# A three-layer transformer kernel on one core: zero fills, first weights and rows on other queues, and odd heads copied by ScalarE

## The reference

```python
# layer 0: focused attention, then a gated mixture of 8 experts, top 2, capacity 560
slot = jnp.where(kept, experts * C + pos, E * C)
buf = jnp.zeros((E * C + 1, D), x.dtype).at[slot].set(xf[tokens])
gu = jnp.einsum('ecd,efd->ecf', xb, w12)
h = jax.nn.silu(g) * u
yb = jnp.einsum('ecf,edf->ecd', h, w3)
...
# layer 2: attention with 16 heads of 64, then 8 experts, top 2, no capacity
y = jax.nn.gelu(flat @ w1[e].T + b1[e], approximate=False)
out = out + y * cw[:, None]
...
return _layernorm(out, ln_w, ln_b)
...
# layer 3: attention with 16 heads of 16 (the narrow one)
scores = jnp.where(mask[:, None, :, :] == 0, jnp.float32(-1000000000.0), scores)
attn = jax.nn.softmax(scores, axis=-1)
```

## Time and profile before

| | us |
|---|---|
| median of 3 runs | 2884.37 (2881.86 to 2885.04) |
| the profiled execution | 2856.36, span 2854.6 |
| PE busy | 2507.7 (88%) |
| DVE busy | 1375.6 (48%) |
| ACT busy | 1158.1 (41%) |
| POOL busy | 801.9 (28%) |

### The profile page before, as it was taken

The page is one execution under the profiler, slowest core; times in us unless marked ns, Lnnn a source line. Parts: engine busy times, 40 slices in busy tenths (PEclk is TensorE's granted clock), DMA queues, the critical chain, the costliest instruction groups (busy, mean ns, idle before and its releaser), DMA issues. The chain is left out here.

```text
span 2854.6 us, 46446 instructions
## 1 busy us (share of the span) xinstructions
PE 2507.7 (88%) x15874; PEld 1765.5 (62%) x15874; DVE 1375.6 (48%) x4867; ACT 1158.1 (41%) x2651; POOL 801.9 (28%) x867
## 2 busy tenths in 40 slices
PE   5999786999986897979999999979899878889776
PEld 4766445888863454647765656556799746656544
DVE  6998511222215654546653333435011078887665
ACT  4556231111107992224444343423333346566331
POOL 3444140000005220017764444514000132222242
PEclk8999897999998998989999999989999969999898
DMA  4232365222105210044210000033888610000000
GB/s 139 76 114 99 122 185 167 90 90 91 53 17 151 69 56 1 1 114 142 109 55 12 7 12 6 1 132 111 298 326 327 241 33 18 18 15 9 1 7 20
DMA packets 71602, 252.17 MB, mean 88 GB/s; under 512 B 16299, under 2 KB 31944, under 8 KB 54912
## 3 DMA queue, kind: packets, MB, share of 16 engines
q1 hardware_dynamic: 61656, 225.71, 23.0%
q0 software_dynamic: 9744, 23.87, 2.8%
HBM read 197.44 MB, written 52.10 MB: 87 GB/s over the span
## 5 line engine op out<-in xcount | busy, mean ns | idle before, releaser
L2889 PE MATMUL L_ffne_up<-L_ffne_xT,L_ffne_wu 128*128 128x128 f32 (+1 forms) x2144 | 390.5, 337 | 7.0 <-DMA L_ffne_wu<-in_L_ffn_up 6.8
L2889 PEld LDWEIGHTS L_ffne_up<-L_ffne_xT,L_ffne_wu 128*128 128x128 f32 x2144 | 328.3, 193 | 54.3 <-DMA L_ffne_wu<-in_L_ffn_up 7.6
L1141 POOL TENSOR_SCALAR L_xattn_p<-L_xattn_p,L_xattn_rec 112x375 f32<-112x375 f32 x256 | 311.8, 1225 | 0.0
L1529 PEld LDWEIGHTS L_xattn_pt<-ident,L_xattn_p 112*125 112x125 f32 x1536 | 202.5, 194 | 164.2 <-issue 78.9
L1529 PE MATMUL L_xattn_pt<-ident,L_xattn_p 112*125 112x112 f32 x1536 | 254.0, 295 | 39.9 <-DVE L_xattn_pt L1378 36.2
L2874 PE MATMUL L_ffne_dn<-L_ffne_wd,L_ffne_hT 128*112 128x256 f32 (+1 forms) x1200 | 266.3, 379 | 1.5 <-issue 1.5
L1361 DVE TENSOR_REDUCE L_xattn_least<-L_xattn_s 112x1 f32<-112x375 f32 x256 | 128.3, 543 | 284.7 <-PE L_xattn_s L1517 284.5
L1378 DVE COPY L_xattn_pt<-L_xattn_pt 125x336 f32<-125x336 f32 x448 | 210.3, 498 | 68.9 <-PE L_xattn_pt L1529 65.7
L2874 PEld LDWEIGHTS L_ffne_dn<-L_ffne_wd,L_ffne_hT 128*112 128x112 f32 (+1 forms) x1200 | 216.8, 183 | 39.7 <-issue 2.1
L2777 POOL DMA_DIRECT2D L_ffn_ybuf<-L_ffne_y x75 | 40.1, 535 | 673.1 <-DVE L_ffne_y L2827 412.2
L1249 ACT ACTIVATE L_xattn_p<-L_xattn_s,L_xattn_least 112x375 f32<-112x375 f32 x256 | 145.1, 570 | 186.2 <-DVE L_xattn_least L1361 186.1
(11 more groups left out here) (364 smaller groups left out, 4509.0 us busy)
## 6 DMA issues: line engine op xcount, KB each, us to landing
L_ffne_wd<-in_L_ffn_down SPq DMA_DIRECT2D x43, 1024.0 KB, 4.8
L_ffne_wu<-in_L_ffn_up SPq DMA_DIRECT2D x35, 1024.0 KB, 5.3
L_ffne_wu<-in_L_ffn_up SPq DMA_DIRECT2D x8, 2048.0 KB, 7.5
L_xattn_kd<-L_xattnkvks SPq DMA_DIRECT2D x8, 1500.0 KB, 7.1
L_xattn_vd<-L_xattnkvvs SPq DMA_DIRECT2D x24, 500.0 KB
L_xattn_kt<-L_xattn_kd SPq DMA_DIRECT2D x8, 1500.0 KB, 6.8
L_xattn_v<-L_xattn_vd SPq DMA_DIRECT2D x8, 1500.0 KB
L_ffn_xbuf<-L_ffnr_zeros SPq DMA_DIRECT2D x8, 1120.0 KB, 13.1
```

The costliest lines, as they stand in the source:

```text
L1141: p = pool.tensor_scalar(at_p(b, head), at_p(b, head), rec[:, h, head:head + 1], None, ALU.mult)
L1529: m = pe.transpose(pt_ps[head % 2][0:KP, 0, kt * S:(kt + 1) * S], at_p(b, head)[:, kt * KP:(kt + 1) * KP], ident[0:S, 0:S])
L2889: m = pe.matmul(up_ps[s % RING][k][:, 0, 0:RH], wu[:, h, c, k * FF + f * 128:k * FF + (f + 1) * 128], xT[:, h, c, q * RH:(q + 1) * RH], st ...
```

## The change

Six things change. (a) The zero fills are issued by ACT, from a 320-column zero tile that lives through the whole program: those of layer 0 in the focused attention at batches 5, 7, 9 and 11, those of layer 2 in the wide attention at batches 8 to 11. xbuf is set up for the whole program, and POOL waits for the fills as before. (b) In routing of layer 0 SP issues wu and wd of expert 0 in the place where the fills stood, into buffers that are held from the program's start. (c) SLOTS is 2. (d) Rows of blocks 0 and 1 of both expert stages are issued by ACT at the stage's start. (e) In the narrow attention ACT copies all odd heads, so each PSUM bank has one engine that empties it. (f) At its start ACT loads the root's table beforehand, on a tiny input, and the bias is added behind the first two batches' `add_experts` and `add_normed`.

```diff
+    def fill(self, eng, pre, q):
+
+        flat = self.xbuf[pre].rearrange("(p n) d -> p (n d)", p=128)
+        eng.dma_start(flat[:, q * 2240:(q + 1) * 2240].rearrange("p (m w) -> p m w", w=320),
+                      self.zeros[:, :].unsqueeze(1).broadcast_to([128, 7, 320])).then_inc(self.filled[pre], 16)
...
+                    if b == FILL_AT[0]:
+                        act.wait_ge(zeros_done, 1)
+                    if b in FILL_AT:
+                        core.fill(act, "L0_ffn", FILL_AT.index(b))
...
-            return not wide and head % 4 == 3
+            return not wide and head % 2 == 1
         def wait_copied(eng, b, head):
             if for_act(head):
-                eng.wait_ge(pt_by_act, b * (H // 4) + head // 4 + 1)
+                eng.wait_ge(pt_by_act, b * (H // 2) + head // 2 + 1)
             elif wide:
                 eng.wait_ge(pt_done, b * H + head + 1)
             else:
-                eng.wait_ge(pt_done, b * (H - H // 4) + head - head // 4 + 1)
+                eng.wait_ge(pt_done, b * (H // 2) + head // 2 + 1)
...
+                else:
+                    act.wait_ge(tiny_done, 1)
+                    act.activation(std3[:, 0:1], tiny[:, :], ACT.Sqrt).then_inc(warm, 1)
+                    act.wait_ge(warm, 1)
...
-                    act.wait_ge(tiny_done, 1)
...
+                    if wide and 8 <= b < 12:
+                        core.fill(act, "L2_ffn", b - 8)
...
+                    copy_pt(NB - 1, H - 3)
                     copy_pt(NB - 1, H - 1)
...
-                    dve.wait_ge(w_in, NLOADS * 16)
                     dve.memset(o_ps[:, 0, :], 0.0).then_inc(pad_done, 1)
-                    dve.wait_ge(bias_out, 1)
-                    dve.tensor_tensor(bias_y[:, :], free_ps[FREE - 1][0:S, 0, 0:D], bias_y[:, :], ALU.add).then_inc(bias_done, 1)
-                    dve.wait_ge(bias_done, 1)
...
+                    dve.wait_ge(w_in, NLOADS * 16)
+                    dve.wait_ge(bias_out, 1)
+                    dve.tensor_tensor(bias_y[:, :], free_ps[FREE - 1][0:S, 0, 0:D], bias_y[:, :], ALU.add).then_inc(bias_done, 1)
+                    dve.wait_ge(bias_done, 1)
...
-    SLOTS = 3
+    SLOTS = 2
...
-                sp.wait_ge(setup, 2)
-                flat = r.xbuf.rearrange("(p n) d -> p (n d)", p=128)
-                for q in range(4):
-                    sp.dma_start(flat[:, q * fill_w:(q + 1) * fill_w], zeros[:, :]).then_inc(filled, 16)
-                sp.wait_ge(filled, 64)
+                if twice:
+                    sp.dma_start(r.wu[:, 0, :, :], ins[pre + "_up"][0]).then_inc(core.early_up, 16)
+                    sp.dma_start(r.wd[:, 0, :, :], ins[pre + "_down"][0]).then_inc(core.early_dn, 16)
...
-                pool.memset(zeros[:, :], 0.0).then_inc(setup, 1)
...
-                pool.wait_ge(filled, 64)
+                pool.wait_ge(core.filled[pre], 64)
...
+        if gated:
+            wu, wd = r.wu, r.wd
...
+            up_in[0], dn_in[0] = core.early_up, core.early_dn
...
-                    after(sp, t_out, (b - 1) * NT)
-                    sp.dma_start(rows[:, h, :, :], r.xbuf[bass.ts(b, R), :].rearrange("(t p) d -> p t d", p=TR)
-                                 ).then_inc(rows_in[h], 16)
-                    after(sp, up_out, (b - 1) * UPB)
-                    sp.dma_start(wu[:, h, :, :], ins[pre + "_up"][e]).then_inc(up_in[h], 16)
-                    after(sp, dn_out, (b - 1) * NT)
-                    sp.dma_start(wd[:, h, :, :], ins[pre + "_down"][e]).then_inc(dn_in[h], 16)
+                    if not isinstance(b, int) or b >= 2:
+                        after(sp, t_out, (b - 1) * NT)
+                        load_rows(sp, b, h)
+                    if not gated or not first(b):
+                        after(sp, up_out, (b - 1) * UPB)
+                        sp.dma_start(wu[:, h, :, :], ins[pre + "_up"][e]).then_inc(up_in[h], 16)
+                        after(sp, dn_out, (b - 1) * NT)
+                        sp.dma_start(wd[:, h, :, :], ins[pre + "_down"][e]).then_inc(dn_in[h], 16)
...
+                load_rows(act, 0, 0)
+                load_rows(act, 1, 1)
...
+                    r.wu = core.sb(kept, pre + "_wu", [128, 2, DC, 2 * FF])
+                    r.wd = core.sb(kept, pre + "_wd", [128, 2, FC, D])
```

More of the change, by code:

```diff
@@ L75, in __init__ @@
         self.shared_in = ctx.enter_context(nc.semaphore("shared_in"))
+        self.filled = {pre: ctx.enter_context(nc.semaphore(f"{pre}_filled")) for pre in ("L0_ffn", "L2_ffn")}
+        self.early_up, self.early_dn = (ctx.enter_context(nc.semaphore(f"early_{n}")) for n in ("up", "dn"))
         self.used = []
@@ L93, in __init__ @@
         self.one = self.sb(ctx, "one", [128, 1])
+        self.zeros = self.sb(ctx, "zeros", [128, 320])
+        self.xbuf = {pre: nc.dram_tensor(pre + "_xbuf", (4480, D), F32).ap() for pre in ("L0_ffn", "L2_ffn")}
     def sb(self, ctx, name, shape, dt=F32):
@@ L194, in hosted @@
                 yield spilled.first + at // PARTS, at % PARTS
+        zeros_done = sem("zeros")
+        FILL_AT = (5, 7, 9, 11)
         with nc.Block() as block:
@@ L245, in _ @@
                 pool.memset(ones[:, :], 1.0).then_inc(setup, 1)
+                pool.memset(core.zeros[:, :], 0.0).then_inc(zeros_done, 1)
                 def normalize(b):
@@ L956, in softmax_attention @@
             got_in = core.got_in["L2_ffn"][0:RING]
+            warm = sem("warm")
             ln_in, tiny_done, summed, var_done, root_done, stats_done = (
@@ L2412, in __init__ @@
         self.owner = core.sb(ctx, pre + "_owner", [1, blocks], I32)
-        self.xbuf = core.nc.dram_tensor(pre + "_xbuf", (rows * blocks, D), F32).ap()
+        assert rows * blocks == 4480
+        self.xbuf = core.xbuf[pre]
         self.ybuf = core.nc.dram_tensor(pre + "_ybuf", (rows * blocks, D), F32).ap()
@@ L2447, in route @@
         ones = sb("ones", [S, S])
-        fill_w = r.R * r.blocks * D // 128 // 4
-        zeros = sb("zeros", [128, fill_w])
         xn4 = sb("xn4", [S, 4, D])
@@ L2469, in route @@
         cum_ps = core.banks(ctx, pre + "r_cum", 2)
-        w_in, std_done, setup, chain, filled = (sem(n) for n in ("w_in", "std", "setup", "chain", "filled"))
+        w_in, std_done, setup, chain = (sem(n) for n in ("w_in", "std", "setup", "chain"))
         xn_done, x_out, x_done, l_out, l_done = (sem(n) for n in ("xn", "x_out", "x", "l_out", "l"))
@@ L2669, in _ @@
                 pe.wait_ge(w_in, NW * 16)
-                pe.wait_ge(setup, 2)
+                pe.wait_ge(setup, 1)
                 def logits(b, h):
@@ L2720, in sem @@
             return core.sem(ctx, pre + "e_" + name)
-        wu, wd = sb("wu", [128, 2, DC, UP]), sb("wd", [128, 2, FC, D])
-        if not gated:
+        if gated:
+            wu, wd = r.wu, r.wd
+        else:
+            wu, wd = sb("wu", [128, 2, DC, UP]), sb("wd", [128, 2, FC, D])
             b1, b2 = sb("b1", [128, 2, FC]), sb("b2", [TR, E, D])
@@ L2747, in last, with load_rows @@
             return isinstance(b, int) and b == N - 1
+        def load_rows(eng, b, h):
+            eng.dma_start(rows[:, h, :, :], r.xbuf[bass.ts(b, R), :].rearrange("(t p) d -> p t d", p=TR)
+                          ).then_inc(rows_in[h], 16)
         with nc.Block() as block:
```

## The result

| | us |
|---|---|
| kernel before, median of 7 runs | 2877.75 (2874.34 to 2885.04) |
| changed kernel, median of 7 runs | 2868.89 (2864.83 to 2872.53) |
| ratio | 0.9956, 95% interval 0.9942 to 0.9970 |
| changed kernel, profiled execution | 2864.83, span 2863.1 |

By the ratio the change makes the kernel 0.44% faster, some 12.7 us of the predicted 34; by the two medians it is 8.9 us. A second comparison on one chip (e11) gives 0.9951. The time stays just outside the range of 2829 to 2868. One thing has to be said of the profile the prediction rested on. It was of an execution of 2856 us, some 21 to 28 us under the medians of the same kernel. I took this as a constant offset. It was not: it sits mostly in the two routings, and it moved the place where the main term was read.

The account below looks back on a forecast made before the run. TensorE was taken as the bound in nearly every stage, so only its idle stretches and half clock counted. Terms −13 − 8 − 1 − 7.2 − 6 + 1 + 0.3 = −33.9 took 2884.37 to 2850 us, range 2829 to 2868.

Parts of the forecast that it names:

- (1): Layer-0 experts: rows land earlier from ScalarE's queue and the wait for wu goes; −13 us (−18 to −2).
- Rival B: Layer-0 experts: rows land no earlier, sharing DMA engines with stores and weights; (1) gives 2.3, total 2861 us; chance 0.13.
- Slots: Layer-0 routing: two slots instead of three cost nothing, with 5.8 us of cover before ScalarE's take of the last values.
- (2): Layer-2 routing: TensorE's 4.55 us stop behind the zero fills goes, with its half-clock restart; −8 us (−9 to −4.5).
- Rival D: Layer-2 routing: the gap stays because tw's 2 MB load holds TensorE; (2) gives about 1, total 2857 us; chance 0.07.
- (3): Layer-2 experts: SyncE starts wu one or two issues sooner; −1 us (−2 to 0) of a 3.78 us wait.
- (4): Narrow attention's start: bias add moved, so VectorE waits only for gathers (−5.9), table loaded beforehand (−1.3); −7.2 us (−8 to −5).
- (5): Narrow loop: ScalarE takes four copies per batch from VectorE, shortening TensorE's copy waits; −6 us (−12 to +5).
- The five large stops: Narrow loop: TensorE's stops like the 3.06 us one, one per two batches, shrink by 0.2 each; −1 us.
- rival A: Narrow loop: half clock after the five stops goes too, 16 us more, total 2834 us; chance 0.13.
- Fills: Focused and wide attention: four fill issues each on ScalarE cost +1 and +0.3 us; bounds 0 and +6.
- Rival C: Narrow loop: ScalarE's order paces TensorE, loop +49, total 2905 us, chance 0.03; weaker form 2861 to 2876, chance 0.07.

Follow-up runs that it names:

- e11: The changed kernel timed again, no edit, on another chip against the kernel before: 2871.65 us, ratio 0.9951.
- e1: The kernel before, profiled again with no edit: 2880.46 us.
- e2: The kernel before with two slots instead of three for spilled keys and values, nothing else: 2884.25 us, ratio 1.0002 to the kernel before.
- e5: The changed kernel with SyncE issuing the rows of blocks 0 and 1 again: 2865.43 us, ratio 0.9934 to the kernel before.
- e6: The changed kernel with SyncE holding layer 0's block 1 weights until block 0's rows have landed: ratio 0.9930 to the kernel before.
- e12: The changed kernel with block 1 weights held until block 0's rows land, beside the changed kernel on one chip: 2857.78 us, ratio 0.9915 to before.
- e3: The changed kernel with three slots, only first halves of wu and wd held early: 2874.90 us, ratio 0.9966 to the kernel before.
- e7: The kernel before with only part (e), ScalarE copying all odd heads: 2877.21 us, ratio 0.9982 to the kernel before.
- e8: The changed kernel without part (e), ScalarE copying every fourth head as before: 2877.10 us, ratio 0.9978 to the kernel before.

## Why the prediction was wrong

**(1) Experts of layer 0: the step that failed.** It said −13 (−18 to −2). Against e1 and e2 it is +6. The removed wait for wu held: 3.3 us in e1, nothing after. What failed is the landing: "I take a landing at 438.5 (11.5 us), nearer the low end, because the rows now lack only a way past the stores". It measured 18.6 us. I asked what the rows had stood behind, and not what had stood behind them. On SyncE's queue they were ahead of the weights. On their own queue they shared the engines with 3 MB of weights issued in the same microsecond, and needed 18.6 us for 11.0 (e5: 10.8 with the rows ahead on SyncE's queue; e6 and e12: 9.9 once the weights wait). Rival B named the weights as competitors but let the rows land no earlier, by the Trainium skill ("DMA: Bandwidth & Descriptors", "Issuing engines are not separate DMA queues"). That section's interleaving agrees with the runs, but "no earlier" was not the worst case: the rows landed 7.6 us later than in e1. My own choice rested on what the Trainium skill says in the same page's "Queues, rings and completion order", rings served in turn; the runs agree with that only in that a second queue gives the rows a share, and no precedence.

The sentence after it failed too: "The load is slow because it stands behind the stores in one queue, not because the engines are full". It was read from 420 to 430 us, but the rows were issued only at 426.95 and landed at 450.00. The weights are issued behind them from 431.33 on, and the windows of the first profile (the last three numbers are granted clock, DMA share and GB/s) show the DMA engines at 0.89 to 1.03 from 435 on:

```profile
430.00:435.00 5.00, 0.00 (x0) 0.00 (x0) 0.00 (x0) 0.00 (x0) 0.00 (x0) 0.50 0.73 225
435.00:440.00 5.00, 0.00 (x0) 0.00 (x0) 0.00 (x0) 0.00 (x0) 0.00 (x0) 0.50 0.94 370
440.00:445.00 5.00, 0.00 (x0) 0.00 (x0) 0.00 (x0) 0.00 (x0) 0.00 (x0) 0.50 0.89 292
445.00:450.00 5.00, 0.01 (x1) 0.01 (x1) 0.00 (x0) 0.00 (x0) 0.00 (x0) 0.50 1.03 278
```

The first profile misled the same term. There TensorE was done at 418 and the rows came only at 450, 23 us after issue. In e1 TensorE is done some 25 us later (442.99), SyncE issues the rows in 0.36 us instead of 4.33, and they land after 11.0 us. So of the 19 us between −13 and +6 some 12 are this start that was read too high (23.0 against 11.0), and 7 are the landing (18.6 against 11.5). I saw the 28 us between profile and median, and carried them over unquestioned. The changed kernel was never timed on a chip where the kernel before takes 2856 us, so what the term gives there is not known.

**Slots**: nothing, shown by e2 and e3.

**(2) Routing of layer 2**: −8 forecast. The stop of 4.55 is gone; in e1 it was 2.04. From the first transpose to the first scatter it is 58.4 us in the first profile, 56.2 and 54.5 in e1 and e2, 51.1 and 52.4 in the changed kernel (e11 the second): −7 against the first profile, −2 to −5 against the others. The mechanism is right, the size was again read from the first profile. To the end of the stage it is 126.2 against 133.0 and 126.7; e1 and e2 differ by 6 us there, with other lengths of the stops during the scatters. Rival D is out.

**(3)** −1 forecast; the wait for wu is 3.47 and 3.62 us (e11 the second) where it was 3.78, and 2.66 in e1 and 3.51 in e2. No gain stands out of the spread.

**(4) Start of the narrow attention**: −7.2 forecast, −5.1 measured from the bias product, −4.6 from the stage's first VectorE work (18.0 against 22.6 us in the first profile). The table load is off the path, −1.3 as forecast. The mis-sized term is the gathers: the second batch's results are added 10.6 us after the stage's first VectorE work (2300.30 to 2310.91), where 8.2 had been worked out with a landing of 2.8 us. VectorE waited for the first batch's gathers, which I had not looked at: the second is through its issue at 2303.26, and VectorE goes on at 2309.19, 5.9 us later. That is near the 6.4 us of my lower bound. The Trainium skill ("ScalarE: Activation LUTs", "What ACT_TABLE_LOAD costs") adds a drain to a switch. It does not show here: the load takes 1.28 us and the first instruction behind it starts within 0.02 us, and so do both loads in the middle of the loop in e1 (1.28 us at 2391.27 and at 2393.07).

**(5) The narrow loop**: −6 forecast, −6.5 to −8.8 measured (e7 against e1 and e2: −8.2). The size is right, the account is not. TensorE's waits for copies were to fall to 28 us plus some on ScalarE's; they are 19.8 and 12.2, no less in all than in e1. The five large stops shrank from about 3.1 to 2.4 to 2.7 us instead of by 0.2, and short ones for ScalarE's copies came in their place. The 8 us stand elsewhere. Over the whole loop of e1 and of e7, which differ by part (e) alone, though on two chips, TensorE's waits for copies are 34.4 and 36.3 us. Its waits for exponentials fall from 4.0 to 0, those for VectorE's minima from 3.1 to 0.5, and its busy time from 333.8 to 330.2, at a granted clock of 0.92 and 0.93. That adds up to −8.3. The changed kernel has the same (36.0, 0, 0.5 and 329.9), and e8 has the old numbers (33.8, 4.1, 2.9 and 335.8). So the gain shows in the waits for exponentials and minima and in the busy time, not in the waits for copies. What shortened those waits was not tested by itself. That the size came out is in part luck. The granted clock stayed 0.96 over 335 us of the loop in both, and the stretches behind the five stops are still below full clock, so rival A did not come.

**Fills**: +1.3 forecast. Routing's first transpose comes at 323.2 against 321.6 in e1, but it lies between 320.4 and 325.6 over all kernels, with and without the fills, so this stays open.

**Rival C** (ScalarE paces TensorE) is out: 12.2 us of waits for its copies, none over 2.2.

The sum by the stretches against the mean of e1 and e2: +6.2 in layer 0, −3.7 in routing 2, −5.1 at the start, −8.4 in the loop, −11 together, with 12.7 by the ratio of times. The stretch from layer 0's first up-product to routing 2 is 5.5 us shorter as well (1434.8), but only 1.0 shorter in e11 (1439.3), so I count it as spread.

## What to carry to other kernels

A load that is moved to a queue of its own loses not only what stood before it but also its place ahead of what stood behind it. Issue the transfer that is waited for first, and hold the large ones back until it has landed: one wait brought the rows 8.5 to 8.8 us sooner here, where the six changes together had brought some 9 to 13 us. And where a profiled execution is 1% off the timed median, profile again before reading waits from it, because the gap may be in the very place that the change touches.

## What the runs showed of the hardware

The stops of TensorE while GpSimd scatters were not expected. Projections stop for 2 to 10 us at a time; in e1 ScalarE's copies start 4.7 to 6.1 us after the product's modelled end, and TensorE's granted clock is 0.50 between the last two stops (406 to 416 us). They appeared in each profile on three of the chips, in all kernels but the one with the late scatter. They are missing in the first profile, although its scatters run beside the projection (374.72 to 413.53). On the fourth chip, where one run of the kernel before took 2855.7 us, no profile has scatters beside the place of the stops. So the same program differs by 1% between chips, by something that needs the scatters. What in the scatters delays the copies, and why only on some chips, stays open; fewer scatters were tried only on the fourth chip.
